# A spectral attention block: the reload of the third-last image pair is issued before the stores of the last pair

## The chip, the cores and the metric

The kernel runs on one NeuronCore of a Trainium2 chip. The metric is the device time of one execution in microseconds (us), and the time of a kernel is the median of several executions. The trace that is read here is of one execution under the profiler.

## The reference

The input x is 4 batches of 64 images of 256x256 float32 (64 MiB); the output has the same shape. Per batch:

```python
x_n   = group_norm(x)                        # here: groups over the last axis, 8 columns each, over all 64 images
k,q,v = spectral convolutions of the normed images, 8 modes each way
att   = softmax(q k^T * scale) v             # attention between the 64 images of the batch
att   = inorm(att) + x_n
mix   = irfft2(rfft2(inorm(att))[32 modes] * mix_w) + skip
out   = x + inorm(inorm(mix)) + att
```

Every output pixel of a batch depends on statistics over all 64 images of that batch. So all images of a batch have to be read and turned into modes before the attention of that batch can begin, and the synthesis of the output comes behind the attention. The four batches are independent of one another.

## The kernel before

One batch (16 MiB) lies whole in SBUF as `X[128, 64, 2, 256]`: image i is `X[:, i]`, two rows of the image to a partition. Two images form a pair (q = 0 to 31), four a quad. X has no second buffer: a batch's results are written over its input in X, stored from there, and then the next batch's images are loaded into the same place.

The program is written out by hand for each engine, with semaphores; no scheduler moves anything. Per batch b there are two parts.

- `attend(b)`: global sums, attention, and the spectral mixing. It starts on VectorE with the sum `SUMS<-Y` (L891), which waits for `y_kept` of all 32 pairs; TensorE meanwhile runs the matmul `psS` of the last quad's squares (L361, `add_squares`) and a few matmuls that compute nothing that is used (L434, `warm`), then multiplies the totals by ones (L440).
- `produce(b)`: for quad after quad the inverse transforms (TensorE L389, ScalarE L576, TensorE L404), the scaling of X (GpSimd L784) and the addition into X (VectorE L836, counted by `out_made`, one count an image). Three quads behind this the next batch's images come in: `forward(b+1, p)` on TensorE (L350) transforms the two images of pair p and waits for the loads of each; ScalarE squares them (L554, `square`) and copies the transform out of PSUM (L546, `keep_y`, counted by `y_kept`), and VectorE sums the squares by group (L872). On ScalarE the order is square, square, `keep_y` for each pair. Behind the last output quad, three quads of forward work are left over (pairs 26 to 31). I call the end of `produce` the seam between two batches; there are three of them, after batch 0, 1 and 2.

All DMAs are issued from SyncE (SP), in one queue. A load has a semaphore `load_done[q]`, a store `store_done[q]`; pairs 0, 30 and 31 are halved (`HALVED`), with one DMA an image and `load_first`, `store_first` for the first image. `store(b, q)` waits for `out_made` and stores (L282). `reload(b+1, q)` waits for the landing of that pair's store and loads the next batch's pair into its place (L278); a wait on SP holds up everything that stands behind it on SP. `batch(b, more)` sets their order: store of pair q, reload of pair q-1, up to pair 29; then the stores of pairs 30 and 31 (four DMAs), then the reloads of pairs 29, 30 and 31 (five DMAs).

Of the kernel before, what the change touches and what calls it, by code (L numbers as in the profile page):

```python
# [14 lines left out]
PAIRS, QUADS, NG = IMGS // 2, IMGS // 4, IMGS // 8  # L15
# [59 lines left out]
def spectral_block(nc, x, mix_re, mix_im, mix_mirror, low_w, low_mix, scalars,  # L75
# [8 lines left out]
    with ctx:  # L84
# [190 lines left out]
        @block.sync  # L275
        def _(sp):
            def load_images(nb, n0, n1, done):
                sp.dma_start(Xf[:, n0:n1, :], x_v[nb, :, n0:n1, :]).then_inc(done, 16)  # L278

            def store_images(b, n0, n1, done):  # L280
                sp.wait_ge(out_made, 64 * b + n1)
                sp.dma_start(out_v[b, :, n0:n1, :], Xf[:, n0:n1, :]).then_inc(done, 16)  # L282

            def load(nb, q):
                if q in HALVED:
                    load_images(nb, 2 * q, 2 * q + 1, load_first[q])
                    load_images(nb, 2 * q + 1, 2 * q + 2, load_done[q])
                else:
                    load_images(nb, 2 * q, 2 * q + 2, load_done[q])

            def reload(nb, q):
                if q in HALVED:
                    sp.wait_ge(store_first[q], 16 * nb)
                    load_images(nb, 2 * q, 2 * q + 1, load_first[q])
                    sp.wait_ge(store_done[q], 16 * nb)
                    load_images(nb, 2 * q + 1, 2 * q + 2, load_done[q])
                else:
                    sp.wait_ge(store_done[q], 16 * nb)
                    load_images(nb, 2 * q, 2 * q + 2, load_done[q])

            def store(b, q):
                if q in HALVED:
                    store_images(b, 2 * q, 2 * q + 1, store_first[q])
                    store_images(b, 2 * q + 1, 2 * q + 2, store_done[q])
                else:
                    store_images(b, 2 * q, 2 * q + 2, store_done[q])

            flat = lambda t: t.rearrange("p r n -> p (r n)")
            small = [(GWT[:, :, :, :, :].rearrange("p a b n v -> p (a b n v)"), t_w), (flat(INVH[:, :, :]), t_inv_h),
                     (INVW[:, :], t_inv_w), (GROUP[:, :], t_group), (EYE[:, :], t_eye), (SEL[:, :], t_sel),  # L310
                     (SIDE[:, :], t_side), (PAIR[:, :], t_pair), (ROWS[:, :], t_rows), (SC[:, :], scalars),
                     (MRE, mix_re), (MIM, mix_im), (MMIR, mix_mirror), (flat(LM[:, :, :]), low_mix),
                     (LW[:, :, :, :].rearrange("p n r k -> p (n r k)"), low_w)]
            sp.dma_start(FWD[:, :, :].rearrange("p a n -> p (a n)"), t_fwd).then_inc(fwd_in, 16)
            for q in range(PAIRS):
                load(0, q)
                for dst, src in small[5 * q - 40:5 * q - 35] if q >= 8 else ():
                    sp.dma_start(dst, src).then_inc(tables_in, 16)  # L318

            def batch(b, more):  # L320
                for q in range(PAIRS - 2):
                    store(b, q)
                    if more and q:
                        reload(b + 1, q - 1)
                for q in range(PAIRS - 2, PAIRS):
                    store(b, q)
                for q in range(PAIRS - 3, PAIRS) if more else ():
                    reload(b + 1, q)

            for b in range(B):  # L330
                batch(b, b < B - 1)
            for q in range(PAIRS):
                sp.wait_ge(store_done[q], 16 * B)
            for q in HALVED:
                sp.wait_ge(store_first[q], 16 * B)
# [852 lines left out]
```

## Time and profile before

| | us |
|---|---|
| median of 3 executions | 677.81 |
| lowest, highest | 675.39, 679.09 |
| the profiled execution | 681.9 |
| its span, first to last instruction | 679.9 |
| busy in it: TensorE / VectorE / GpSimd / ScalarE | 636.5 / 487.8 / 356.1 / 334.3 |
| bytes read and written | 68.23 MB, 67.11 MB |

The profiled execution is 4.1 us above the median and 2.0 us above its own span. A span is cut into instructions by engine; "PE" is TensorE's matmuls, "DVE" VectorE, "ACT" ScalarE, "SPq" an issue or a wait of SyncE. The three seams lie at about 215 to 233, 380 to 397 and 543 to 561 us of the span.

### The profile page before, as it was taken

How to read it: one execution, taken by the hardware profiler on the slowest of the kernel's cores; microseconds unless marked ns; L12 is line 12 of the kernel's file. 1: busy time of each engine (PE TensorE's matmuls, PEld its weight loads, DVE VectorE, ACT ScalarE, POOL GpSimd, SP SyncE). 2: the span in 40 equal slices, each digit the busy share in tenths (PEclk: the TensorE clock that was granted, in tenths of full speed). 3: DMA queues.
4: the chain of work that ended last, by engine and by line, in shares of the span. 5: the costliest groups of instructions: out<-in, count | busy, mean ns of one | idle time of the engine just before them, and what ended most of it. 6: DMA issues, size and time to landing. Idle time of an engine off the chain costs nothing.

```text
span 679.9 us, 15103 instructions
## 1 busy us (share of the span) xinstructions
PE 636.5 (94%) x5736; PEld 581.6 (86%) x5736; DVE 487.8 (72%) x1099; ACT 334.3 (49%) x722; POOL 356.1 (52%) x430
## 2 busy tenths in 40 slices
PE   9999999899999799979999899989999989995984
PEld 9999998699999799869999789969899988994863
DVE  4667676688777567668777666857887666778896
ACT  6888142465666413255666523246566650433331
POOL 0350035959960013796993002398799000359995
PEclk9999999899999899999999999999999989999997
DMA  9990000998999200299999900059989960004786
GB/s 320 350 379 9 1 2 20 308 314 294 310 318 328 94 1 1 77 308 343 286 328 309 322 14 1 2 198 331 321 285 325 308 218 1 1 1 162 280 302 247
DMA packets 72071, 136.32 MB, mean 200 GB/s; under 512 B 5760, under 2 KB 6272, under 8 KB 72000
## 3 DMA queue, kind: packets, MB, share of 16 engines
q1 hardware_dynamic: 72000, 135.36, 58.5%
q8 instruction: 46, 0.75, 0.4%
q14 instruction: 25, 0.20, 0.1%
HBM read 68.23 MB, written 67.11 MB: 199 GB/s over the span
## 4 chain that ended last, share of the span: by engine, by line
PE 58%; DVE 15%; POOL 9%; DMA 8%; issue 3%; ACT 3%; SPq 3%; POOLq 0%; DVEq 0%; ACTq 0%
PE psY L350 23%; PE psP L404 12%; POOL X L784 7%; PE psY L373 6%; DMA X<-in_x 6%; PE psT L389 5%; PE psP L454 5%; DVE QP L872 4%; ACT SQ L554 2%; PE psP L373 2%; DVE Y L836 2%; DVE SQ L836 2%; DMA out<-X 2%; SPq L318 2%; DVE X L836 1%
## 5 line engine op out<-in xcount | busy, mean ns | idle before, releaser
L350 PE MATMUL psY<-FWD,X 128*128 128x128 f32 x2048 | 251.1, 281 | 17.5 <-DMA X<-in_x 17.4
L350 PEld LDWEIGHTS psY<-FWD,X 128*128 128x128 f32 x2048 | 238.8, 195 | 33.0 <-issue 33.0
L784 POOL TENSOR_TENSOR X<-X,ALPHA 128x512 f32<-128x512 f32 x244 | 254.7, 1080 | 21.7 <-DVE IM L1072 19.7
L872 DVE TENSOR_REDUCE QP<-SQ 128x32 f32<-128x512 f32 x256 | 162.1, 679 | 57.8 <-ACT SQ L554 57.8
L836 DVE TENSOR_TENSOR X<-X,psP 128x512 f32<-128x512 f32 x192 | 126.5, 684 | 59.9 <-PE psP L404 26.1
L554 ACT ACTIVATE SQ<-X 128x512 f32<-128x512 f32 x256 | 146.4, 622 | 21.1 <-DMA X<-in_x 14.4
L404 PE MATMUL psP<-INVW,T 64*128 64x256 f32 x768 | 141.3, 402 | 12.0 <-DVE X L836 11.3
L762 POOL TENSOR_TENSOR Y<-Y,OMEGA 128x256 f32<-128x256 f32 x32 | 25.3, 790 | 215.9 <-ACT Y L558 215.6
L404 PEld LDWEIGHTS psP<-INVW,T 64*128 64x128 f32 x768 | 92.9, 190 | 31.2 <-issue 16.0
L576 ACT ACTIVATE T<-psT,BIA,SCL 128x256 f32<-128x256 f32 x128 | 65.3, 560 | 110.3 <-PE psT L389 105.8
L546 ACT ACTIVATE Y<-psY 128x512 f32<-128x512 f32 x128 | 76.2, 596 | 60.4 <-PE psY L350 59.6
L373 PE MATMUL psY<-GWR,Y 128*128 128x128 f32 x768 | 93.2, 279 | 0.0
L373 PEld LDWEIGHTS psY<-GWR,Y 128*128 128x128 f32 x768 | 87.8, 192 | 4.1 <-issue 3.0
L404 PE MATMUL psB<-INVW,T 64*128 64x256 f32 x256 | 69.7, 393 | 0.0
L389 PE MATMUL psT<-INVH,Y 64*128 64x256 f32 x512 | 67.1, 378 | 0.0
L389 PEld LDWEIGHTS psT<-INVH,Y 64*128 64x128 f32 x512 | 51.3, 189 | 4.8
L767 POOL TENSOR_TENSOR Y<-Y 128x256 f32<-128x256 f32 x32 | 23.8, 743 | 47.1 <-DVE Y L836 47.1
L404 PEld LDWEIGHTS psB<-INVW,T 64*128 64x128 f32 x256 | 46.1, 188 | 0.0
L836 DVE TENSOR_TENSOR X<-X,psB 128x512 f32<-128x512 f32 x64 | 43.6, 682 | 3.1 <-POOL X L784 2.6
L454 PEld LDWEIGHTS psP<-GWR,Y 128*64 128x64 f32 x272 | 30.5, 204 | 2.4 <-DVE GWR L839 2.4
L563 ACT ACTIVATE Y<-Y 128x128 f32<-128x128 f32 (+2 forms) x44 | 12.9, 294 | 39.4 <-DVE Y L836 28.5
L454 PE MATMUL psP<-GWR,Y 128*64 128x64 f32 x272 | 31.1, 275 | 0.8 <-DVE GWR L839 0.8
(189 smaller groups left out, 478.8 us busy)
## 6 DMA issues: line engine op xcount, KB each, us to landing
X<-in_x SPq DMA_DIRECT2D x116, 512.0 KB, 5.5
out<-X SPq DMA_DIRECT2D x116, 512.0 KB, 4.4
X<-in_x SPq DMA_DIRECT2D x24, 256.0 KB, 5.2
out<-X SPq DMA_DIRECT2D x24, 256.0 KB, 3.7
INVH<-t_inv_h SPq DMA_DIRECT2D x1, 256.0 KB, 9.6
LW<-in_low_w SPq DMA_DIRECT2D x1, 204.0 KB, 6.6
GWT<-t_w SPq DMA_DIRECT2D x1, 192.0 KB, 9.9
FWD<-t_fwd SPq DMA_DIRECT2D x1, 128.0 KB, 2.1
```

What stands on the lines that cost most here:

```text
L350: last = mm(psY[p % 2][:, (2 * i + c) * 128:(2 * i + c + 1) * 128], X[:, 2 * p + i, a, c * 128:(c + 1) * 128], FWD[:, a, :], start=a == 0, ...
L373: last = mm(over(psM[g % 3][:, col:col + 1], [[256, 2], [1, 64]]), both[:, c, k, :], over(GWR[:, c, k, 0, 0:1], [[NV, 2], [1, 2 * NV]]), s ...
L389: last = mm(psT[h][:, 0:H], S[rows, q, part, :, :].rearrange("p j n -> p (j n)"), INVH[rows, part, :], start=part == 0, stop=part == 1)
L404: last = mm(out_bank(b, 2 * s + i)[:, W * a:W * (a + 1)], T[rows, s % 4, 128 * a:128 * (a + 1)], INVW[rows, :], start=True, stop=True)
L454: last = mm(ps[0:IMGS, col:col + 64], Y[:, c, k, :, U0 + n], GWR[:, c, 0, k:k + 2, :], start=c == 0, stop=c == WC - 1)
L546: nc.scalar.activation(Y[:, :, :, i0:i0 + 3:2, :].rearrange("p c k i u -> p i (c k) u"), psY[p % 2][:, :].rearrange("p (i n u) -> p i n u" ...
L554: nc.scalar.activation(SQ[:, n % RING, :], Xf[:, n, :], ACT.Square).then_inc(squared, 1)
L576: nc.scalar.activation(T[:, p % 4, :], psT[p % 2][:, 0:H], ACT.Identity, bias=BIA[:, p:p + 1], scale=SCL[:, p:p + 1]).then_inc(t_kept, 1)
L762: P.tensor_tensor(v, v, over(OMEGA[:, 0:1], [[0, 4], [0, 2], [1, NV]]), MUL).then_inc(powers_weighted, 1)
L784: P.tensor_tensor(v, v, al, MUL).then_inc(x_scaled, 1)
L836: return V.tensor_tensor(out, a, b, op)
L872: V.tensor_reduce(QP[:, 4 * (k % 2) + place(n) % 4, :], SQ[:, n % RING, :].rearrange("p (a g j) -> p g a j", a=HC, j=GW), AX.XY, ADD).then ...
```

## The change

The order on SP at the end of a batch changes, and nothing else: no instruction is added or taken away, on any engine.

```diff
             def batch(b, more):
-                for q in range(PAIRS - 2):
+                for q in range(PAIRS):
                     store(b, q)
                     if more and q:
                         reload(b + 1, q - 1)
-                for q in range(PAIRS - 2, PAIRS):
-                    store(b, q)
-                for q in range(PAIRS - 3, PAIRS) if more else ():
-                    reload(b + 1, q)
+                if more:
+                    reload(b + 1, PAIRS - 1)
```

SP's instructions at a seam, before. `X<-in_x` is a load, `out<-X` a store; 128x2x512 is a pair, 128x512 one image; each row tells the semaphore it waits for.

```order
L278 DMA X<-in_x 128x2x512 [waits store_done28]
L282 DMA out<-X 128x512 [waits out_made] x4
L278 DMA X<-in_x 128x2x512 [waits store_done29]
L278 DMA X<-in_x 128x512 [waits store_first30]
L278 DMA X<-in_x 128x512 [waits store_done30]
L278 DMA X<-in_x 128x512 [waits store_first31]
L278 DMA X<-in_x 128x512 [waits store_done31]
```

The same place in the changed kernel:

```order
L278 DMA X<-in_x 128x2x512 [waits store_done28]
L282 DMA out<-X 128x512 [waits out_made] x2
L278 DMA X<-in_x 128x2x512 [waits store_done29]
L282 DMA out<-X 128x512 [waits out_made] x2
L278 DMA X<-in_x 128x512 [waits store_first30]
L278 DMA X<-in_x 128x512 [waits store_done30]
L278 DMA X<-in_x 128x512 [waits store_first31]
L278 DMA X<-in_x 128x512 [waits store_done31]
```

The load of pair 29, with its wait for the store of pair 29, has moved past the two stores of pair 31. The last batch has no reloads and keeps its order.

## Rows read from the trace of the kernel before

**Rows 1.** The page's parts 4 (chain by engine) and 5 (count | busy us, mean ns | idle before):

```profile
PE 58%; DVE 15%; POOL 9%; DMA 8%; issue 3%; ACT 3%; SPq 3%; POOLq 0%; DVEq 0%; ACTq 0%
...
L546 ACT ACTIVATE Y<-psY 128x512 f32<-128x512 f32 x128 | 76.2, 596 | 60.4 <-PE psY L350 59.6
```

**Rows 2.** Chain of waits, first seam: start us, us, what:

```profile
218.88 5.86 DMA X<-in_x
...
224.88 3.35 PE psY L350 x16
...
230.57 0.02 ACT Y L546
...
233.50 0.97 PE psP L434 x4
234.47 0.18 PE psT L440 x2
```

**Rows 3.** Chain of waits, second and third seam:

```profile
384.48 6.08 DMA X<-in_x
...
547.39 6.04 DMA X<-in_x
```

**Rows 4.** Timeline, TensorE at the three seams: start us, us, instruction [idle before]:

```profile
224.88 3.35 PE L350 MATMUL psY<-FWD,X 128*128 128x128 f32 x16 [2.54 <-DMA X<-in_x]
...
390.69 2.02 PE L350 MATMUL psY<-FWD,X 128*128 128x128 f32 x16 [3.23 <-DMA X<-in_x]
...
553.57 3.38 PE L350 MATMUL psY<-FWD,X 128*128 128x128 f32 x16 [2.60 <-DMA X<-in_x]
```

**Rows 5.** Timeline, VectorE behind the three seams:

```profile
232.99 0.37 DVE L891 TENSOR_REDUCE SUMS<-Y 128x2 f32<-128x128 f32 x1
233.88 0.24 DVE L839 TENSOR_SCALAR T<-SEL,SUMS 128x32 f32<-128x32 f32 x1
...
397.18 0.37 DVE L891 TENSOR_REDUCE SUMS<-Y 128x2 f32<-128x128 f32 x1
...
561.41 0.37 DVE L891 TENSOR_REDUCE SUMS<-Y 128x2 f32<-128x128 f32 x1
```

**Rows 6.** Timeline of SP's issues, stores of pair 29 and of images 61, 62:

```profile
212.16 0.52 SPq L282 DMA_DIRECT2D out<-X  x1
...
217.11 0.36 SPq L282 DMA_DIRECT2D out<-X  x1
217.71 0.33 SPq L282 DMA_DIRECT2D out<-X  x1
...
377.28 0.41 SPq L282 DMA_DIRECT2D out<-X  x1
...
540.79 0.42 SPq L282 DMA_DIRECT2D out<-X  x1
```

**Rows 7.** DMA issues at 211.3:212.6, 376.7:377.6, 540.2:541.1 us; last column: us to landing:

```profile
X<-in_x SPq DMA_DIRECT2D x1, 512.0 KB, 5.5
out<-X SPq DMA_DIRECT2D x1, 512.0 KB, 6.0
...
out<-X SPq DMA_DIRECT2D x1, 512.0 KB, 6.7
...
out<-X SPq DMA_DIRECT2D x1, 512.0 KB, 6.3
```

**Rows 8.** Timeline of SP's issues, the load of pair 27, then that of image 63:

```profile
211.38 0.72 SPq L278 DMA_DIRECT2D X<-in_x  x1
...
222.08 0.33 SPq L278 DMA_DIRECT2D X<-in_x  x1
```

**Rows 9.** DMA issues at 216.5:218.8 and 220.1:222.2 us:

```profile
out<-X SPq DMA_DIRECT2D x4, 256.0 KB, 3.7
...
X<-in_x SPq DMA_DIRECT2D x4, 256.0 KB, 5.2
```

**Rows 10.** Busy time by stretch, first seam: PE, PEld, DVE, ACT, POOL, PEclk, DMA, GB/s:

```profile
225.40:228.60 3.20, 3.20 (x17) 3.20 (x16) 1.28 (x2) 0.85 (x2) 0.00 (x0) 0.50 0.09 29
```

## The prediction

> **What bounds the kernel now.** I read the page first: TensorE carries 58% of the chain that ended last and DMA 8% [rows 1]. A change of SP's order can only touch the DMA part, so the next view is the chain of waits around each of the three seams. At the first it goes over a load issued at 218.88, which takes 5.86 us to land, and then to TensorE at 224.88 [rows 2]. This is the load of pair 29, the first of the five behind the stores: TensorE has just finished pair 28 and stands idle for 2.54 us until it lands. At the second and third seam the same load takes 6.08 and 6.04 us [rows 3], and TensorE stands idle for 3.23 and 2.60 us [rows 4]. So about 8.4 us of the span are this one wait, three times. From the landing on the kernel works through pairs 29, 30 and 31 and reaches `SUMS<-Y`, the start of the next attention, at 232.99, 397.18 and 561.41 [rows 5]. These three times are my yardstick: nothing of the attention can start before, and everything behind moves with them. In the second seam the way from the landing (384.48 + 6.08 = 390.56) to SUMS takes 6.6 us; in the first it takes 8.25 and in the third 8.0, because TensorE runs pair 29 in 3.35 and 3.38 us there against 2.02 [rows 4], at a granted clock of 0.50 [rows 10], which is 1.2 GHz of its two levels 1.2 and 2.4.
>
> **What the change removes.** The load of pair 29 no longer stands behind the two stores of pair 31. It might go as soon as SP has issued image 61's store, at 217.11 + 0.36 = 217.5 [rows 6], 1.4 us earlier than now. But its wait moves with it: it needs the landing of pair 29's store. That store is issued at 212.16, 377.28 and 540.79 [rows 6] and takes 6.0, 6.7 and 6.3 us [rows 7], so it lands at 218.2, 384.0 and 547.1. The load is issued then, earlier by only 0.7, 0.5 and 0.3 us.
>
> How long it takes is not in the trace for this place. The lower end is 5.2 us, the refills of one image with little ahead of them [rows 9]; the upper end is the 6.1 us that the second seam shows with four stores just ahead [rows 3]. The load of pair 27, with one store ahead, took 5.5 [rows 7]. Two image stores will be ahead, which is between; I take 5.6. Pair 29 then lands at 223.8, 389.6 and 552.7, earlier by 0.9, 1.0 and 0.7 us. If the way from there to SUMS stayed as short as in the second seam, that would be a clear gain.
>
> **What the change adds.** Two things are now behind the load that were ahead of it: the stores of images 62 and 63, and with them the reloads into their place.
>
> First SP itself. Image 62's store went out at 217.71 [rows 6]; now it is queued behind SP's wait until 218.2 and the load's issue, so it goes out about 1 us later. Alone that is harmless, since that store has no other reader than the reload.
>
> Second the DMA queue. A load of a pair is issued at 211.38 [rows 8] and lands after 5.5, at 216.9; the store of a pair issued 0.8 us behind it, at 212.16, lands after 6.0, at 218.2 [rows 7]: 1.3 us after the load. A store with only stores ahead takes 3.7 [rows 9]. So a store behind a load lands after the load has, plus the time of its bytes, 1.3 us for 512 KB. The two stores of pair 31 together are 512 KB. They landed at about 221.5 and 222.1 before (222.08 is when SP could issue the last reload [rows 8]); now they land 0.65 and 1.3 us after the load of pair 29: at 225.1, 390.9 and 554.0 for image 63, some 3 us later than before.
>
> The refills follow from that. Each takes 5.2 us [rows 9]: image 62 of the next batch lands at 223.8 + 0.65 + 5.2 = 229.7, image 63 at 230.3 (before, 222.08 + 5.2 = 227.3, well ahead of TensorE). TensorE finishes pairs 29 and 30 at 223.8 + 0.14 + 4.0 = 227.9, where 0.14 is the step from the landing to the first matmul at 224.88 [rows 2], and now stands idle for pair 31 instead, about 1.9 us. What is late next is therefore the last pair's load.
>
> **The sum.** From the landing of image 62 to SUMS: 0.14 to the matmul, 2.02 for the pair at full clock [rows 4], 0.6 for ScalarE's copy (mean 596 ns [rows 1]), which in the trace before starts right at the pair's end, and a few hundredths to hand over: 2.8 us. From the landing of pair 29's store to SUMS in all: 5.6 + 0.65 + 5.2 + 2.8 = 14.3 us. That gives SUMS at 232.5, 398.3 and 561.4, against 232.99, 397.18 and 561.41: -0.5, +1.1 and 0.0, together +0.6 us.
>
> One small gain lies behind it. Now the idle warming matmuls (L434) run from 233.50 to 234.47, and the totals' matmul L440 starts only then [rows 2], though VectorE had its input ready at 233.88 + 0.24 = 234.1 [rows 5]. In the changed kernel the squares of the last images are summed while TensorE still works on pair 31, so the warming matmuls start earlier and L440 waits for VectorE alone: 0.3 us less at each seam, -0.9 us.
>
> Together -0.3 us: 681.6 us for an execution such as the profiled one with its 681.9. The median before is 677.81, 4.1 us lower, and I carry the difference over: **677.5 us**. With the load at its ends of 5.2 and 6.1 us instead of 5.6 the three seams give -1.5 and +1.2 us, so this case alone spans about 676.3 to 679.0. The rest costs nothing: SP has no other work while it waits, the pair 30 reloads still wait for stores that were issued ahead of the load, and the last batch keeps its order.
>
> **Rival one: the gain comes through.** The last pair's loads would have to land by 227.9, when TensorE is through with pair 30, so 1.8 us sooner than I count, and then the end hangs on pair 29 alone. With 6.6 us from its landing to SUMS the three seams give 230.4, 396.2 and 559.3: -2.6, -1.0 and -2.1, together -5.7 us, 672.1. If the slow clock stays as it is, only the earlier landings count, -0.9, -1.0 and -0.7: 675.2. I call it 673.5. For it speaks that DMA engines move 512 KB in 1.3 us, so that bytes are not short; against it that a store lands 1.3 us behind its load in the rows, and that four refills in a row took 5.2 us each. A chance of 17%.
>
> The Trainium skill's page "DMA: Bandwidth & Descriptors" (section on the anatomy of one DMA, SWDGE path) gives a DMA as about 2.0 us plus its bytes at 436 GB/s. By that an estimate for the refill of one image is 2.6 us, the last pair would be there by 227.1, and this rival would be the outcome; the trace has 5.2 us for it, and I go by the trace.
>
> **Rival two, slower: the slow clock moves behind the seam.** TensorE's idle time before pair 29 shrinks to 1.5, 2.3 and 1.9 us, and a second one of 1.9 us stands directly ahead of pair 31, with the serial attention behind it. If the clock falls there as it did at the first and third seam, the half-speed stretch (at least 3.2 us at 0.50 [rows 10]) lies on the chain and costs half of itself, 1.6 us a seam: +4.8 - 0.3 gives 682.3; at two seams of three 680.7; with the load at 6.1 us up to 683.8. I call it 682. It decides whether 1.9 us of idle are enough: the clock fell at idle times of 2.54 and 2.60 us and not at 3.23 [rows 4], so length alone doesn't settle it. A chance of 21%.
>
> The skill's page "TensorE: Matmul & The Clock Gate" (section on HAM oscillation) has it that DMA waits between bursts of matmuls throttle the clock again when they are long; by it two short waits in place of a long one would rather spare the slow stretch. The trace agrees only in part, with 3.23 us of idle and no fall.
>
> **Rival three: the load isn't really ahead.** Pair 29's store might land so late that the load goes out at the same time as now, with SP's stores held up as well. It is the case above with its upper end, since the issue moves by 0.3 to 0.7 us at most: 677.5 to 679. It is in the forecast's share.
>
> **Chances.** The forecast's case 62%, the gain 17%, the slow clock 21%. A measurement of this kernel can tell about 0.5% from no change, 3.4 us: faster is below 674.4, slower above 681.2. Most of the gain's case lies below (16%), most of the slow case above (19%), which leaves 65% for no difference. The range takes in half of either rival: 673.5 to 682.0.
>
> **What the trace of the changed kernel would show.** SP: the load of pair 29 at the moment its store lands, and image 62's store behind it. That store and image 63's land 0.65 and 1.3 us after the load of pair 29, where 3.7 us from issue would prove me wrong. TensorE: two idle times at each seam, one before pair 29 and one before pair 31. If the second is missing, rival one holds; if a granted clock of 0.50 stands behind it, rival two does. A SUMS that comes 14.3 us after the landing of pair 29's store would bear out the sum.

## The result and the profile after

The changed kernel takes 672.86 us (median of 8 executions, 669.28 to 676.75) against 678.69 us for the kernel before (median of 8, 675.39 to 684.08). The ratio is 0.9897 with a 95% interval of 0.9862 to 0.9932: about 1.0% or 5.8 us faster. The forecast was 677.5 us and no difference that can be measured; the outcome is rival one, which I had given 17%, and the time lies just below my range (673.5 to 682.0). The execution profiled here took 676.75 us, the longest of the eight; a second profile of the same kernel, used further down, is of one that took 669.88 us, the shortest of nine.

The page of the changed kernel, its first line and the chain by engine:

```profile
span 674.7 us, 15103 instructions
PE 55%; DVE 16%; DMA 12%; POOL 9%; ACT 4%; issue 3%; SPq 0%; POOLq 0%; DVEq 0%; ACTq 0%
```

The chain's DMA share has grown from 8% [rows 1] to 12%, though the kernel is faster. So the share says where the chain runs, not what it costs. The timeline of TensorE shows the cost (start us, us, instruction, [idle before]); these are the forward transforms (L348 in the changed file) of pairs 29, 30 and 31 at the first seam, of pairs 29 and 31 at the second, and of pair 29 at the third:

```profile
221.56 2.02 PE L348 MATMUL psY<-FWD,X 128*128 128x128 f32 x16 [1.36 <-DMA X<-in_x]
223.56 2.03 PE L348 MATMUL psY<-FWD,X 128*128 128x128 f32 x16
225.77 2.02 PE L348 MATMUL psY<-FWD,X 128*128 128x128 f32 x16 [0.18 <-DMA X<-in_x]
...
385.49 1.24 PE L348 MATMUL psY<-FWD,X 128*128 128x128 f32 x9 [0.51 <-DMA X<-in_x]
...
389.77 2.02 PE L348 MATMUL psY<-FWD,X 128*128 128x128 f32 x16 [0.25 <-DMA X<-in_x]
...
549.88 2.53 PE L348 MATMUL psY<-FWD,X 128*128 128x128 f32 x13 [2.10 <-DMA X<-in_x]
```

The idle times ahead of pair 29 were 2.54, 3.23 and 2.60 us before [rows 4], 8.4 us together; now they are 1.36, 0.51 and 2.10, together 4.0. The second idle time that I had forecast, 1.9 us ahead of pair 31, is 0.18 us at the first seam, 0.25 at the second and absent at the third. The chain of waits at the first seam shows why (start us, us, what). It now runs over the store and the reload of image 62:

```profile
214.86 1.08 DVE X L834 x2
215.94 6.13 DMA out<-X
222.07 0.02 issue
222.09 3.55 DMA X<-in_x
225.64 0.14 issue
225.77 2.04 PE psY L348 x16
227.81 0.02 issue
227.83 0.61 ACT Y L544
228.44 0.02 issue
228.46 0.38 DVE SUMS L889
```

Everything here is as I counted it (the store held behind the load of pair 29, then the reload, 0.14 us, 2.04 us, 0.61 us) except one number: the reload lands 3.55 us after its issue, not 5.2. The DMA issues of SP at the three seams, with the time to landing in the last column: first the load of pair 29 at each seam, then the two stores of pair 31 at the first, then the last two reloads at each:

```profile
X<-in_x SPq DMA_DIRECT2D x1, 512.0 KB, 5.9
...
X<-in_x SPq DMA_DIRECT2D x1, 512.0 KB, 5.3
...
X<-in_x SPq DMA_DIRECT2D x1, 512.0 KB, 5.6
...
out<-X SPq DMA_DIRECT2D x2, 256.0 KB, 6.1
...
X<-in_x SPq DMA_DIRECT2D x2, 256.0 KB, 3.5
...
X<-in_x SPq DMA_DIRECT2D x2, 256.0 KB, 3.6
...
X<-in_x SPq DMA_DIRECT2D x2, 256.0 KB, 3.4
```

Not all of the difference between the two profiled executions is the change's. SUMS stands at 228.46, 392.46 and 558.0 against 232.99, 397.18 and 561.41 [rows 5]: 4.5, 4.7 and 3.4 us earlier, which doesn't grow from seam to seam as the change's gain alone would. From the third SUMS to the end of the span, where nothing was changed, the kernel before took 679.9 - 561.4 = 118.5 us and this one 116.7; that 1.8 us of the 5.2 us between the spans isn't the change's. The clock adds to it. Where TensorE waits for pair 1's load at the start of a batch, which the change doesn't touch, two stretches at half clock followed in the changed kernel's execution (at 291 and 455 us) and one in that of before (at 130 us). With those at the seams (one now, two before) each execution has three up to its third SUMS, so this profile doesn't show by itself that the change saves such stretches. From the busy time by stretch of the changed kernel (columns as in [rows 10]):

```profile
221.50:225.00 3.50, 3.44 (x31) 3.47 (x32) 1.45 (x3) 2.48 (x5) 0.00 (x0) 1.00 0.72 255
550.60:553.90 3.30, 3.30 (x17) 3.30 (x17) 1.11 (x2) 1.13 (x3) 0.00 (x0) 0.50 0.48 171
291.20:294.50 3.30, 3.30 (x17) 2.99 (x17) 2.09 (x4) 0.96 (x2) 3.30 (x5) 0.50 0.93 287
```

So the medians carry the verdict, and the traces are read for the steps.

### The profile page after: what moved, and what is told of

It is laid out like the page before. It is cut to its first block, busy times and chain, and to the rows that moved or that the text cites. A ratio compares the mean times of both kernels' runs of the same rounds, so it can differ in the third digit from the quotient of the medians.

```text
span 674.7 us, 15103 instructions
## 1 busy us (share of the span) xinstructions
PE 638.3 (95%) x5736; PEld 581.3 (86%) x5736; DVE 487.6 (72%) x1099; ACT 334.6 (50%) x722; POOL 356.5 (53%) x430
## 4 chain that ended last, share of the span: by engine, by line
PE 55%; DVE 16%; DMA 12%; POOL 9%; ACT 4%; issue 3%; SPq 0%; POOLq 0%; DVEq 0%; ACTq 0%
PE psY L348 21%; PE psP L402 11%; POOL X L782 7%; DMA out<-X 7%; PE psY L371 6%; DMA X<-in_x 5%; PE psT L387 5%; PE psP L452 5%; DVE QP L870 5%; ACT SQ L552 3%; DVE Y L834 2%; PE psP L371 2%; DVE SQ L834 2%; DVE X L834 1%; DVE IM L841 1%
## 5 line engine op out<-in xcount | busy, mean ns | idle before, releaser
L348 PE MATMUL psY<-FWD,X 128*128 128x128 f32 x2048 | 250.2, 280 | 14.1 <-DMA X<-in_x 13.5
L348 PEld LDWEIGHTS psY<-FWD,X 128*128 128x128 f32 x2048 | 237.3, 194 | 30.2 <-issue 27.2
L387 PE MATMUL psT<-INVH,Y 64*128 64x256 f32 x512 | 68.8, 386 | 0.0
L402 PE MATMUL psB<-INVW,T 64*128 64x256 f32 x256 | 68.3, 387 | 0.0
```

Source lines behind the costliest of these rows:

```text
L348: last = mm(psY[p % 2][:, (2 * i + c) * 128:(2 * i + c + 1) * 128], X[:, 2 * p + i, a, c * 128:(c + 1) * 128], FWD[:, a, :], start=a == 0, ...
L387: last = mm(psT[h][:, 0:H], S[rows, q, part, :, :].rearrange("p j n -> p (j n)"), INVH[rows, part, :], start=part == 0, stop=part == 1)
L402: last = mm(out_bank(b, 2 * s + i)[:, W * a:W * (a + 1)], T[rows, s % 4, 128 * a:128 * (a + 1)], INVW[rows, :], start=True, stop=True)
```

## Experiments

I went in with theory Q: the gain is that pair 29's load has 512 KB less ahead of it in the queue, and the last reloads took 5.2 us before only because they were queued themselves. Its rivals were S (only SP's issue times or waits matter) and C (the gain is the slow clock that goes). All ratios are to the kernel before, run beside it on the same chip.

**One of the two stores ahead.**

```diff
-                for q in range(PAIRS - 2, PAIRS):
-                    store(b, q)
-                for q in range(PAIRS - 3, PAIRS) if more else ():
+                store(b, PAIRS - 2)
+                store_images(b, IMGS - 2, IMGS - 1, store_first[PAIRS - 1])
+                if more:
+                    reload(b + 1, PAIRS - 3)
+                store_images(b, IMGS - 1, IMGS, store_done[PAIRS - 1])
+                for q in range(PAIRS - 2, PAIRS) if more else ():
                     reload(b + 1, q)
```

> One of the two stores of pair 31 (image 62) is ahead of the load of pair 29, the other (image 63) behind it. Theory Q (queue): what the change gains is that pair 29's load lands sooner because 512 KB of stores no longer stand ahead of it; with one image store ahead, half of the gain goes: the load lands some 0.65 us later than in the changed kernel, and the time is about 675 to 676 us, between 678.7 and 672.9. Theory S (issue): what counts is only when SP issues the load, which is the landing of pair 29's store here too; then the time is that of the changed kernel, 673. Theory C (clock): the gain is the slow-clock stretches that are gone; half the shortening of TensorE's idle time may be enough for that, 673 to 679.

Measured: 675.5 us, ratio 0.9954 (0.9926 to 0.9981), half of the changed kernel's gain. TensorE's idle times ahead of pair 29 in its timeline, together 5.0 us, lie between the 8.4 and the 4.0:

```profile
223.40 0.79 PE L353 MATMUL psY<-FWD,X 128*128 128x128 f32 x5 [1.16 <-DMA X<-in_x]
386.26 0.91 PE L353 MATMUL psY<-FWD,X 128*128 128x128 f32 x6 [2.12 <-DMA X<-in_x]
549.02 1.24 PE L353 MATMUL psY<-FWD,X 128*128 128x128 f32 x9 [1.69 <-DMA X<-in_x]
```

That is Q's number; S had given 673. But S took it that the load goes out as soon as pair 29's store has landed, and in this trace it goes out 1.10, 0.13 and 0.45 us later, hardly sooner than before (0.69, 0.53 and 0.34). So the run shows that a load issued as late as before gains when one store less is ahead of it: it lands 5.3 to 5.8 us after its issue, where it took 5.9 to 6.1. It doesn't show that the issue time is worth nothing. In the changed kernel's first profile both got shorter, by about 0.5 us (issue) and 0.4 us (flight) a seam.

**The load ahead of pair 30's stores too.**

```diff
+                if more:
+                    reload(b + 1, PAIRS - 3)
                 for q in range(PAIRS - 2, PAIRS):
                     store(b, q)
-                for q in range(PAIRS - 3, PAIRS) if more else ():
+                for q in range(PAIRS - 2, PAIRS) if more else ():
                     reload(b + 1, q)
```

> The load of pair 29 goes ahead of the stores of pair 30 too. SP must wait for pair 29's store before it can issue them, so they go out about 1 to 1.5 us late. Theory Q: the load lands some 1.5 to 2 us earlier than in the changed kernel and TensorE's idle time before pair 29 is gone, but then pair 30's loads come late and TensorE waits there instead: within 1.5 us of the changed kernel, 671.5 to 674.5. Theory S (SP's wait is what costs): the held-up stores make the whole seam later, 675 or more. Theory C: idle times are short in any case, so as the changed kernel.

Measured: 681.6 us, ratio 1.0051 (1.0029 to 1.0074), slower than the kernel before. This is S's number, and I had given Q 671.5 to 674.5. The chain of waits at its second seam:

```profile
378.47 5.83 DMA out<-X
384.30 0.01 issue
384.32 0.37 SPq L278
384.68 0.04 issue
384.73 4.26 DMA out<-X
388.99 0.02 issue
389.01 3.81 DMA X<-in_x
392.81 0.14 issue
392.95 5.45 PE psY L352 x32
398.40 0.02 issue
398.42 0.61 ACT Y L548
```

Four steps now follow each other that overlapped before: pair 29's store (5.83), SP's wait for it and the load's issue, image 60's store (4.26), and its reload (3.81). TensorE waits for pair 30 then, 2.80, 2.40 and 1.63 us at the three seams. At the second seam it takes 5.45 us over two pairs which take 4.0 at full clock, and the stretches by time show the half clock at both the first and second seam:

```profile
227.00:230.30 3.30, 3.30 (x18) 3.30 (x17) 1.14 (x3) 1.56 (x4) 0.00 (x0) 0.50 0.03 11
394.30:397.50 3.20, 3.20 (x17) 3.20 (x16) 1.29 (x3) 1.63 (x3) 0.00 (x0) 0.50 0.02 6
```

Here is what I had feared for pair 31, at pair 30: SP's wait, and the slow clock behind a late idle time; no run parts the two. A load can be too early. In the changed kernel pair 29's store has landed by the time SP has issued pair 30's stores, or lands within 1.2 us of it. Here SP reaches that wait at 381.1, some 3.2 us before the landing at 384.30, stands in it, and the stores behind it go out late.

**Filling TensorE's idle time, in the order of before and in the changed order.** `warm(n)` issues n matmuls whose result isn't used; the diff is that of the order of before, and the changed order has `warm(2)` in the same place.

```diff
+                        if u == QUADS + 1:
+                            pe.wait_ge(out_made, 64 * b + 64)
+                            warm(5)
                         forward(b + 1, 2 * (u - LAG) + 1)
```

> The order of before, with five warming matmuls (about 2.4 us, their result isn't used) in TensorE's idle time ahead of pair 29. They change no data and no DMA. Theory C (clock): most of the 5.8 us gained by the change is the slow clock, so this kernel comes to 673 to 675. Theory Q: a slow stretch costs 1.4 to 1.6 us where it falls, and the profiled execution of before had two of them at the seams, so at most 3 us go: 675.5 to 677.5, and the load of pair 29 still lands where it did.

> The changed kernel with two warming matmuls (0.97 us) ahead of pair 29. In the order of before, five of them gained 2.1 us in the median (ratio 0.9969). Theory Q with the clock as a part: the changed kernel's shorter idle time leaves less for the clock to lose, so the filling gains 1 us or nothing: 671.5 to 673.5. Rival C (the clock is still the larger part in both orders): again 2 us or more, below 671.

Measured: in the order of before 676.56 us, ratio 0.9969 (0.9943 to 0.9994); in the changed order 672.80, ratio 0.9898 (0.986 to 0.9936), which is the changed kernel's own 0.9897. So about 0.3% or 2 us of the gain could be had without touching a DMA, by keeping the clock up (the interval reaches from 0.06% to 0.57%), and in the changed order no such gain can be measured. The stretches of the filled kernel in the old order at its three seams, each with a mean granted clock of 1.00:

```profile
219.70:227.00 7.30, 7.30 (x59) 7.04 (x58) 4.07 (x7) 4.35 (x9) 0.00 (x0) 1.00 0.59 207
382.00:391.50 9.50, 8.72 (x68) 8.05 (x66) 4.61 (x9) 5.40 (x11) 0.00 (x0) 1.00 0.45 157
545.00:554.50 9.50, 9.33 (x74) 9.10 (x75) 5.25 (x10) 6.18 (x12) 0.00 (x0) 1.00 0.62 212
```

With the idle time filled in both, the change still makes 0.9898 / 0.9969 = 0.993, some 4.8 us or 1.6 us a seam. C falls as the main cause and stays as about a third of the gain. It may be a little more: in the old order the unused matmuls end 0.4 and 0.2 us after pair 29 could have started at the first and third seam, so the filling has a small cost of its own. The quotient is of two separate comparisons and has no interval of its own.

**A small load in pair 29's place.** The order of before; the reload of pair 29 brings 16 of each image's 512 columns, so the next batch is computed from the old contents for the rest of that pair, and its output differs.

```diff
+                elif q == PAIRS - 3:
+                    sp.wait_ge(store_done[q], 16 * nb)
+                    sp.dma_start(Xf[:, 2 * q:2 * q + 2, 0:16], x_v[nb, :, 2 * q:2 * q + 2, 0:16]).then_inc(load_done[q], 16)
```

> The order of before, but the load of pair 29 at the seams brings 16 of the 512 columns of each of its two images (16 KB in place of 512 KB); the rest of pair 29 keeps the previous batch's output, so the result differs. It asks what the 5.2 us of the last refills were. Theory Q: they were time in the queue behind pair 29's load; without its bytes each refill of an image lands 3.5 to 4 us after its issue. Rival L: a load's own latency is 5.2 us, and they stay at 5.2. The time falls by 2 to 3 us a seam either way, since TensorE no longer waits for pair 29.

Measured: 666.61 us (one execution), 12.5 us or 4 us a seam below the kernel before beside it, where I had expected 2 to 3 a seam. The four reloads behind it, at the three seams, each row with the median of the four:

```profile
X<-in_x SPq DMA_DIRECT2D x4, 256.0 KB, 3.5
...
X<-in_x SPq DMA_DIRECT2D x4, 256.0 KB, 2.9
...
X<-in_x SPq DMA_DIRECT2D x4, 256.0 KB, 3.3
```

With 512 KB less ahead of them the same four reloads, issued in the same order on the same waits, take 2.9 to 3.5 us in the median (2.6 to 3.8 one by one) instead of 5.2 [rows 9]. This settles what the 5.2 us were: some 1.7 to 2.3 us of it was waiting behind pair 29's bytes. Rival L is out.

**The load from GpSimd's queue.** SP keeps the order of before, without pair 29's reload; GpSimd, idle there, waits for pair 29's store and issues the load itself (with a semaphore of its own, for which TensorE and ScalarE wait from the second batch on).

```diff
+                if b < B - 1:
+                    q = PAIRS - 3
+                    pool.wait_ge(store_done[q], 16 * (b + 1))
+                    P.dma_start(Xf[:, 2 * q:2 * q + 2, :], x_v[b + 1, :, 2 * q:2 * q + 2, :]).then_inc(pool_load, 16)
```

> SP keeps the order of before, all four stores together, but the load of pair 29 is taken from SP and issued by GpSimd, which is idle there, as soon as pair 29's store has landed. So it is ahead of or beside pair 31's stores in time, without SP waiting and in another queue. Theory Q (queued bytes and not SP's wait): the load shares the DMA engines with pair 31's stores, lands about as in the changed kernel, and the refills of the last pair don't stand behind it: 671 to 673.5. Rival S (the order within SP's queue is what gives the gain): the load gets half of the engines and lands as late as before, 677 to 679.

Measured: 679.71 us, ratio 0.999 (0.9963 to 1.0018), no gain. The profiled execution is the shortest of the twelve, 674.76 us, so its idle times are those of a good one. At the first seam the load is issued at 217.18, 0.3 us after the landing of its store, and takes 6.9 us; at the second and third it takes 5.7 and 6.1:

```profile
X<-in_x POOLq DMA_DIRECT2D x1, 512.0 KB, 6.9
...
X<-in_x POOLq DMA_DIRECT2D x1, 512.0 KB, 5.7
...
X<-in_x POOLq DMA_DIRECT2D x1, 512.0 KB, 6.1
```

TensorE idles 2.78, 1.56 and 2.15 us for it. From the landing of pair 29's store to the landing of the load it is 7.3, 6.0 and 6.4 us, against 6.6, 6.6 and 6.4 before and 5.9, 5.3 and 5.6 in the changed kernel. The time is that of the rival: an issue that doesn't wait for SP gains nothing while the stores of pair 31 are in the other queue at the same time, on the same DMA engines. Against S it says that an earlier issue alone isn't enough; against my number for Q (671 to 673.5), that beside the stores isn't ahead of them. Whether the load lost to the stores of the other queue or to GpSimd's own way of issuing a DMA (its issue took 0.95 us at the first seam) is open; the same load from ScalarE's queue wasn't tried.

**Halving pair 29 as well.** On top of the changed kernel:

```diff
-HALVED = (0, PAIRS - 2, PAIRS - 1)
+HALVED = (0, PAIRS - 3, PAIRS - 2, PAIRS - 1)
```

> The changed kernel with pair 29 halved too: its store and its load are one DMA an image, as those of pairs 30 and 31 are. Theory Q: the first image's store is issued one addition earlier and its load needs only 256 KB in place of 512 KB, so TensorE can start pair 29 some 0.6 to 1.2 us sooner where it still idles (1.36, 0.51 and 2.10 us in the changed kernel's trace): 1 to 3 us in all, 670 to 672. Theory S: SP has two DMAs and waits more in the same place, which costs 0.5 us a seam, so 673 to 675.

Measured: 671.75 us, ratio 0.9884 (0.9849 to 0.9918). Repeated beside the changed kernel on one chip:

> The changed kernel with pair 29 halved, again, beside the changed kernel on one chip. Measured before: 671.75, ratio 0.9884. Theory Q: 1 us or a little more below the changed kernel in the same call; if it is no lower, the halving is not worth anything.

> The changed kernel again, beside the others on one chip, and for a second profile. Measured before: 672.86, ratio 0.9897. Theory Q: the load of pair 29 lands 5.3 to 6 us after its issue, the refills of pair 31 within 3.4 to 3.8 us of theirs, and no granted clock of 0.50 stands behind the two idle times of a seam except by chance; theory of the prediction: 5.2 us for the refills.

Measured: halved 671.24, ratio 0.9869 (0.9826 to 0.9913); changed 673.59, ratio 0.9908 (0.9875 to 0.994). It is lower both times, by 1.1 us (each against its own runs of the kernel before) and 2.4 us (beside each other), but the intervals overlap: the fastest version tried that computes the whole result, and not shown beyond doubt to beat the changed kernel. Both beat the kernel before. TensorE's longest idle times for a load at the seams of the halved kernel's first profile are 0.43, 1.05 and 0.45 us. Only the 1.05 is still ahead of pair 29; the other two are ahead of pair 30, whose first image lands 0.14 us before TensorE goes on. In the second profile all three (0.40, 0.48 and 0.46 us) are ahead of pair 30. So what is late next is pair 30.

The changed kernel's second profile has idle times of 0.28, 0.50 and 0.51 us ahead of pair 29 and no half clock at any seam:

```profile
218.00:228.00 10.00, 9.25 (x81) 8.87 (x79) 7.46 (x13) 7.85 (x15) 0.00 (x0) 1.00 0.64 216
380.00:389.00 9.00, 8.31 (x73) 8.01 (x71) 6.40 (x11) 6.92 (x14) 0.00 (x0) 1.00 0.65 231
541.00:550.00 9.00, 8.19 (x73) 7.94 (x71) 6.52 (x11) 7.05 (x14) 0.00 (x0) 1.00 0.62 220
```

**The same move at the start of a batch.** The halved kernel, with the load of pair 1 ahead of the store of pair 2:

```diff
                     store(b, q)
-                    if more and q:
+                    if more and q and q != 2:
                         reload(b + 1, q - 1)
+                    if more and q == 1:
+                        reload(b + 1, q)
```

> The changed kernel with pair 29 halved, and the same move at the start of a batch: the load of pair 1 goes ahead of the store of pair 2, where TensorE idles 1.8 to 2.8 us for pair 1's load (126.28 to 128.04 us in the trace of the halved kernel). Theory Q: the load lands up to 1.3 us earlier, the bytes of one pair's store, and 1 to 1.3 us go at each of three batch starts: 668 to 670 where the halved one has 671.75. Rival: pair 2's load, whose store is now held up by SP's wait, comes late in turn, as pair 30's did when the load of pair 29 went ahead of its store; then 671 to 674.

> As the kernel before it (pair 29 halved, pair 1's load ahead of pair 2's store), with pair 1 halved too. Theory Q: pair 1's store is issued one image earlier and its first image's load needs 256 KB only, so 0.6 us more at each batch start: 666.5 to 669. Rival: two more issues and waits on SP hold up pair 2's store: no better than the kernel before it.

Measured, beside those two repeats: 674.8, ratio 0.9922 (0.9891 to 0.9953), where the halved kernel has 0.9869; with pair 1 halved too 671.79, ratio 0.9871 (0.9825 to 0.9917). The move is worth nothing there: the first is 3.6 us above the halved kernel, with intervals that overlap, and the second level with it. At the second batch start TensorE still waits for pair 1, and now for pairs 2 and 3 as well:

```profile
290.94 2.02 PE L350 MATMUL psY<-FWD,X 128*128 128x128 f32 x16 [2.51 <-DMA X<-in_x]
296.33 2.02 PE L350 MATMUL psY<-FWD,X 128*128 128x128 f32 x16 [0.17 <-DMA X<-in_x]
299.47 0.80 PE L350 MATMUL psY<-FWD,X 128*128 128x128 f32 x5 [1.12 <-DMA X<-in_x]
```

At a seam the stores that are passed are the last ones and nothing needs them soon. At the start of a batch the queue runs on for some 95 us, and a store that waits delays the loads behind it; that this is why the move fails there is my reading, and no run isolates it.

## Why the prediction was wrong

- **What bounds the seam** held: the load of pair 29 and TensorE's wait for it. So did what SP does: the load goes out at the landing of its store (215.51 after a landing at 215.49 in the changed kernel), and the two stores of pair 31 take 5.2 to 6.1 us behind it, where they took 3.7 [rows 9].
- **The failed step is "Each takes 5.2 us"**, the refill of an image. I read it as a latency, and even as the lower end for a load with little ahead of it. A good part of it, about 1.7 us, was queueing: the small load brought it to 2.9 to 3.5 us, and in the changed kernel, where only a store and two reloads of one image are still in flight at its issue, it is 3.4 to 3.6. The trace before could have told. At the first seam pair 29's load landed at 224.74, and the reload issued 1.3 us behind it at 225.41, just the 0.65 us later that its bytes take; the other three followed at 0.65 us each. That is what a queue at its rate looks like. (The equal spacing alone isn't: they were issued 0.65 us apart as well, which a fixed latency would show too.) I counted the stores behind a load in just this way, and not the reloads. Nor had the four stores, with their 3.7 us, "only stores ahead": the load of pair 28 was in flight until 219.51, and image 60's store landed 0.6 us after it. With 3.5 in place of 5.2, my own sum puts image 62's landing at 228.0 where TensorE needs it at 227.9: the second idle time shrinks from 1.9 us to nothing, as the trace has it (0.18 us at that seam), and 1.7 us a seam come back, 5 us in my own sum.
- **The page that I set aside was nearer.** By the Trainium skill's "DMA: Bandwidth & Descriptors" (anatomy of one DMA, which is there for DMAs issued from GpSimd, where these are SyncE's) I had an estimate of 2.6 us for such a refill, and named rival one as its outcome. The measured refills of pair 31 in the changed kernel are 3.4 to 3.6 us in the first profile and 2.7 to 3.4 in the second; with the small load the four reloads took 2.6 to 3.8 (the shortest is image 60's, issued at 379.62 us). That is mostly longer than the page's sum, but near the point that decided, 3.4 us, which is 1.8 less than I counted. I weighed a fitted fixed cost against a row and took the row, without asking what stood in the queue in that row.
- **The load of pair 29** was sized right. I took 5.6 us from issue; it took 5.9, 5.3 and 5.6 in the first profile of the changed kernel, and 4.1, 4.5 and 5.2 in the second. Counted from the landing of pair 29's store it landed 0.9 us a seam earlier in the first profile, as forecast. The idle time ahead of it fell by 1.5 us a seam there (8.4 to 4.0 in three), because TensorE was also done with pair 28 some 0.6 us later against that store than before; why is open.
- **The sum as a whole** had 14.3 us from the landing of pair 29's store to SUMS. It was 14.8, 13.2 and 14.4 us before; in the changed kernel it is 13.0, 12.4 and 13.8 in the first profile and 11.0, 11.2 and 12.6 in the second. That is 3.1 and 7.6 us less over three seams, on either side of the 5.8 us of the medians. So the 5.2 accounts for the missed gain in size, but the single execution varies by as much as the gain.
- **The clock.** I had priced the slow stretch only as it might move behind the seam. What happened is the other side: where the idle time is filled the slow stretch at the seam is gone, and that is worth 0.3%. The rule on long DMA waits in the Trainium skill's "TensorE: Matmul & The Clock Gate" (section on HAM oscillation) pointed that way. The filled kernels agree with its direction; the single idle times don't order by length, since the clock fell after 2.54, 2.60 and 2.10 us and not after 3.23. Rival two wasn't wrong as a mechanism: in the kernel with the load ahead of both pairs it is part of the loss, at 1.0051.
- **The small gain at L440**, 0.3 us a seam, can't be told from noise. In the changed kernel's first seam this matmul (L438 there) starts at 229.65, 1.2 us behind SUMS at 228.46, where it was 1.5 [rows 2, 5], so it came at that seam.
- **Rival one's time**, 673.5 with 672.1 for the full gain, is the one that came. Its full gain was 5.7 us and 5.8 were measured; that they agree so closely is partly luck, as the profiles scatter by several us.

## What to carry to other kernels

A time from issue to landing is a latency only if nothing was ahead in the queue. Before using it as a floor, look at what landed just before: a DMA that lands behind its forerunner by no more than the time of its own bytes was queued. That issues and landings have the same spacing says nothing. When a few last stores and loads share one queue, put a load that an engine waits for ahead of stores that nobody waits for, but not so early that the issuing engine stands in its wait with stores behind it that are needed: one place further forward turned a gain of 1.0% into a loss of 0.5%. Idle time on TensorE can cost twice, by its length and by the clock behind it.

## What I had not expected of the hardware

- A load issued from GpSimd's queue beside the stores of pair 31 in SP's took 6.9, 5.7 and 6.1 us at the three seams, about as long as the 5.9, 6.1 and 6.0 us of the same load behind all four stores in SP's queue [rows 2, 3]. Being in another queue it no longer held up the store behind it, though: at the first and third seam image 63's store, issued 0.3 and 0.05 us after the load, landed 2.0 and 2.5 us before it, where in one queue it landed 1.3 us after the load at every seam of the changed kernel.
- The reload of an image with no load of a pair just ahead of it took anything from 2.6 us (second seam with the small load) to 3.8 us (third seam of the same run). I know no cause for the spread.
